# A vision tower on one core: B row split by TensorE, shares repeated by DMA, weights loaded ahead

## What is computed

```python
xn = layernorm(h); xz = xn @ W_in.T; x_main, z = split(xz)
xm = silu(conv4(x_main)); Bt = xm @ W_B.T; Ct = xm @ W_C.T
dt = softplus(xm @ W_dt.T + b_dt)                       # softplus = max(x,0) + log(1+exp(-|x|))
h[t] = exp(A*dt)*h[t-1] + dt*Bt*xm                      # 16 states, 256 channels
y = (h*Ct).sum(states); h1 = h0 + (y*silu(z)) @ W_out.T
# 8 experts, each takes its 1024 best rows of all (softmax over rows), gelu MLP, scatter-add
# last: tokens rolled by 32, attention over the 8 heads of one token (q.k of head h and head g),
#       output dealt out again and projected, then:
u = layernorm(h3); out = h3 + shared(u) + sum_e share[e] * (W_ex[e] @ swiglu(w_up @ u)) + biases
# share: one of 2 groups, the best 2 of its 4 experts, normalized
```

## Time and profile before

| | |
|---|---|
| median of three runs | 2949.59 us |
| the profiled execution | 2955.88 us, span 2954.1 us |
| busy, share of the span | PE 83%, DVE 83%, POOL 67%, ACT 51% |
| mean granted clock of TensorE | 0.924 |
| scan stage | 0 to about 1580 us |
| middle | to about 1922 us |
| last stage | to the end |

### The profile page before, as it was taken

One profiled execution on the slowest core, in us unless ns is written; L12 is line 12 of the kernel. 1 busy time (PEld: TensorE's weight loads), 2 busy tenths in 40 slices (PEclk: granted clock), 3 DMA queues, 4 the chain that ended last, 5 costly groups with the idle time before them and its releaser, 6 DMA issues. The chain is left out here.

```text
span 2954.1 us, 25221 instructions
## 1 busy us (share of the span) xinstructions
PE 2455.6 (83%) x6718; PEld 1146.3 (39%) x6718; DVE 2447.7 (83%) x3527; ACT 1511.1 (51%) x2542; POOL 1978.0 (67%) x1008
## 2 busy tenths in 40 slices
PE   6899898898998898988973068438999999998998
PEld 2344444444444444444431033213444444444443
DVE  4999999999999999999997822137888888888875
ACT  5666666666666666676652134234444433443332
POOL 3888888888888887888882068755555555555540
PEclk9999999999999999999996579758999999999999
DMA  2333323323333323324231024310000000000000
GB/s 83 110 94 98 109 92 105 106 87 117 94 99 107 100 91 108 103 87 119 89 102 51 0 50 71 36 51 22 29 29 29 29 29 29 29 29 29 26 22 11
DMA packets 169758, 199.27 MB, mean 67 GB/s; under 512 B 38969, under 2 KB 156946, under 8 KB 169490
## 3 DMA queue, kind: packets, MB, share of 16 engines
q1 hardware_dynamic: 158354, 189.27, 20.9%
q0 software_dynamic: 11264, 8.40, 2.2%
HBM read 164.37 MB, written 33.25 MB: 67 GB/s over the span
## 5 line engine op out<-in xcount | busy, mean ns | idle before, releaser
L905 POOL TENSOR_TENSOR a_hc<-a_h,a_cs 128x896 f32<-128x896 f32 (+1 forms) x448 | 891.6, 2002 | 182.1 <-DVE a_h L744 181.2
L360 PE MATMUL a_y_bank<-a_hc,a_ident 128*128 128x448 f32 (+1 forms) x1792 | 766.7, 562 | 14.7 <-POOL a_hc L905 13.6
L537 ACT ACTIVATE a_da<-a_dt,a_neg_a 128x448 f32<-128x448 f32 (+1 forms) x896 | 548.4, 632 | 331.3 <-DVE a_h L744 330.3
L744 DVE TENSOR_TENSOR_SCAN a_h<-a_da,a_h,a_dbx 128x448 f32<-128x448 f32 x528 | 583.1, 1134 | 14.2 <-ACT a_da L537 11.9
L360 PEld LDWEIGHTS a_y_bank<-a_hc,a_ident 128*128 128x128 f32 x1792 | 344.1, 196 | 359.9 <-issue 287.2
L2086 POOL TENSOR_TENSOR c_prod<-c_prob,c_qkv 128x1024 f32<-128x1024 f32 x100 | 280.7, 2849 | 274.6 <-DVE c_prob L1973 274.6
L1670 PE MATMUL c_p_ACC<-c_sc,c_w_ex 128*128 128x512 f32 x800 | 365.4, 594 | 0.0
L2079 POOL TENSOR_TENSOR c_prod<-c_qkv 128x1024 f32<-128x1024 f32 x100 | 231.9, 2341 | 152.7 <-ACT c_qkv L1754 152.7
L728 DVE TENSOR_TENSOR a_dbx<-a_dtx,a_b_bank 128x896 f32<-128x896 f32 (+1 forms) x308 | 328.5, 1067 | 4.5 <-PE a_b_bank L353 0.7
L1947 DVE TENSOR_TENSOR c_sc<-c_hid,c_p_CB 128x1024 f32<-128x1024 f32 x200 | 239.9, 1214 | 69.6 <-PE c_p_CB L1662 67.1
L893 POOL TENSOR_TENSOR a_dbp<-a_dtx,a_bs 128x896 f32<-128x896 f32 (+1 forms) x140 | 269.7, 1936 | 0.3
(11 more groups left out here) (297 smaller groups left out, 3688.3 us busy)
## 6 DMA issues: line engine op xcount, KB each, us to landing
a_cs<-c_rows SPq DMA_DIRECT2D x96, 896.0 KB, 5.3
a_bs<-c_rows SPq DMA_DIRECT2D x24, 1120.0 KB, 5.7
a_cs<-c_rows SPq DMA_DIRECT2D x16, 900.0 KB, 4.4
c_x<-h_rows SPq DMA_DIRECT2D x25, 256.0 KB, 2.8
heads<-c_ot SPq DMA_DIRECT2D x25, 256.0 KB, 2.3
c_dealt<-heads SPq DMA_DIRECT2D x200, 32.0 KB, 1.9
rolled<-c_res SPq DMA_DIRECT2D x25, 256.0 KB, 2.1
h_rows<-a_th SPq DMA_DIRECT2D x24, 224.0 KB
```

The lines of the kernel that those rows point to most:

```text
L360: pe.matmul(y_bank[:, d, 0:g.w], ident[:], hc[:, (g.i * NS + n) % HC_RING, d, 0:g.w], start=(n == 0), stop=(n == NS - 1)).then_inc(s_sum, 1)
L537: act.activation(da[:, k % DA_RING, 0:g.w], dt[g.slot][:, d, 0:g.w], ACT.Exp, scale=neg_a[:, d * NS + n:d * NS + n + 1]).then_inc(s_da, 1)
L744: dve.tensor_tensor_scan(h[:, n, d, 0:g.w], da[:, (g.i * 2 * NS + k) % DA_RING, 0:g.w], x, state, ALU.mult, ALU.add).then_inc(s_scan, 1)
L905: pool.tensor_tensor(hc[:, (q.i * NS + n) % HC_RING, :, 0:q.w], h[:, n, :, 0:q.w], cs[:, n % C_RING, 0:q.w].unsqueeze(1).to_broadcast([P, ...
```

## The change

**Scan stage.** The bank that holds B and C stays open. ScalarE rounds it to `bc` (high part); TensorE then adds minus the high part into the same bank, by a matmul with a negated identity (`less_high`); ScalarE rounds the rest (`middle_b`), TensorE takes that off too (`less_middle`), ScalarE rounds the low part (`low_b`). `split_b` and `low_b` are gone from VectorE, and `one_more` is ScalarE's. `trh` moves to bank 0, `logit` to bank 1, and all four order lists are new.

**Middle.** GpSimd clears its lists only when VectorE has made the keys. Ahead of expert 2's weights SyncE loads the last stage's weights into tiles that live through both stages (`fixed_tiles`); VectorE clears a bias tile in round 6 of the search and does the small preparations behind its middle work.

**Last stage.** The shares go to DRAM as 8 rows and come back repeated over all 128 partitions, in two transfers of 1 MB; `spread(e)` and its banks are gone. The hidden expert rows lie in PSUM (`hx`). The biases of choice and shared part are one bf16 matmul. x is transposed into the bank ahead of the projection. The order lists are new.

```diff
-              ("dt1", 0, 1), ("out", 0, -1), ("trh", 1, -1), ("cen2", 0, -1), ("var2", 1, -1), ("tok", 1, 2),
-              ("logit", 0, -1), ("cen", 0, 2), ("var", 1, 2), ("trn", 1, -1))
+              ("dt1", 0, 1), ("out", 0, -1), ("trh", 0, -1), ("cen2", 0, -1), ("var2", 1, -1), ("tok", 1, 2),
+              ("logit", 1, -1), ("cen", 0, 2), ("var", 1, 2), ("trn", 1, -1))
...
+            def less_high():
+                if p:
+                    pe.wait_ge(s_bch, p.i + 1)
+                    pe.matmul(tile_of("bc", p)[:, 0:p.w], less[:, 0, :], bc[p.slot][:, 0:p.w], start=False, stop=True,
+                              skip_group_check=True).then_inc(s_less, 1)
...
+            def low_b():
+                if p:
+                    act.wait_ge(s_less, 2 * p.i + 2)
+                    act.copy(bc[p.slot][96:128, 0:p.w], tile_of("bc", p)[96:128, 0:p.w]
+                             ).then_inc(s_free[nth["bc", p.i][0]], 1)
+
+            def one_more():
+                if p:
+                    act.wait_ge(s_spe, p.i + 1)
+                    need(act, s_spm, p.i)
+                    act.activation(yt[:, :, 0:p.w], spe[:, :, 0:p.w], ACT.Identity, bias=1.0).then_inc(s_spu, 1)
...
-            def split_b():
...
-            def low_b():
...
-            def one_more():
...
+            if e == 2:
+                progs["c_load"](sp)
             need(sp, s_out, 2 * (e - 1))
...
+            if r == 6:
+                progs["c_clear"](dve)
...
     def gpsimd(pool):
         after_a(pool)
+        pool.wait_ge(s_dve, progs["n_high"])
         pool.memset(ones[:], 1.0).then_inc(s_fill, 1)
...
+            def share_out():
+                if X is not None:
+                    sp.wait_ge(s_c_s, X + 1)
+                    sp.dma_start(share_rows[X % 2], c_s[SHARE:SHARE + E1, :]).then_inc(s_rows[X % 2], 16)
+
+            def share_in():
+                if X is not None:
+                    sp.wait_ge(s_rows[X % 2], (X // 2 + 1) * 16)
+                    for half in range(2):
...
+                        sp.dma_start(c_all[:, r, :, :], share_rows[X % 2][half * EG:(half + 1) * EG, :].partition_broadcast(P)
+                                     ).then_inc(s_all[r], 16)
+
+            load()
+            share_out()
+            heads_out()
+            store_last()
+            share_in()
+            heads_in()
...
-            def spread(e):
...
+                    product = hid[U % 2][:, i, :] if i < 2 else hx[:, i - 2, :]
...
+                    dve.tensor_tensor(sc[:, n % SC_RING, :, :], hx[:], shares(dve, X, e), ALU.mult
+                                      ).then_inc(s_sc, 1)
...
             exp_table()
+            gate_exp()
+            row_scale()
+            score_exp()
             keep_h3()
-            score_exp()
             square()
-            row_scale()
+            column_scale()
             norm_rows()
-            column_scale()
-            gate_exp()
+            affine()
             silu_table()
-            affine()
```

More of the change, by code:

```diff
@@ L1 @@
 from contextlib import ExitStack
+from dataclasses import dataclass
 import numpy as np
@@ L851, in vector @@
             scans(6, 1)
-            split_b()
+            scans(7, 0)
             product(8)
-            scans(7, 0)
             scans(7, 1)
@@ L857, in vector @@
             scans(8, 0)
+            scans(8, 1)
             product(10)
-            scans(8, 1)
             scans(9, 0)
+            scans(9, 1)
             product(11)
-            scans(9, 1)
-            one_more()
-            low_b()
-            lost()
             scans(10, 0)
@@ L1435, in bank_table @@
     return nth
-def phase_c(nc, ctx, mem, a, h_rows, out, after_b, progs):
+SHARE, PARTS = 96, (0, 32, 64)
+KB = PARTS[-1] + E1 + 1
+@dataclass
+class Fixed:
+    ident: object
+    cen_w: object
+    mean_w: object
+    w_qkv: object
+    w_proj: object
+    w_up: object
+    w_so: object
+    w_ex: object
+    w_gate: object
+    gate_b: object
+    cols: object
+    eps_cols: object
+    earlier: object
+    later: object
+    bias9: object
+    bias_b: object
+    cc: object
+    s_in: object
+    s_const: object
+    loads: int
@@ new lines, in sync, with load, store, store_last @@
+        for X, U, N, A, L in turns:
+            def load():
+                if L is not None:
+                    if L >= 3:
+                        result(sp, "proj", L - 3)
+                    sp.dma_start(x[L % 3][:], h_rows[L * GW + SHIFT:(L + 1) * GW + SHIFT, :].rearrange(
+                        "(j p) d -> p j d", p=P)).then_inc(s_x[L % 3], 16)
+            def store(c):
+                if c is not None and c >= 0:
+                    taken(sp, "acc", c)
+                    sp.dma_start(out[:, c * GW:(c + 1) * GW], res[c % 2][:]).then_inc(s_res[c % 2], 16)
+            def store_last():
+                if X:
+                    store(X - 1)
+            def heads_out():
+                if N is not None:
+                    taken(sp, "o", N)
+                    sp.dma_start(heads[N % 2], ot[:]).then_inc(s_heads[N % 2], 16)
+            def heads_in():
+                if N is not None:
+                    s = N % 2
+                    sp.wait_ge(s_heads[s], (N // 2 + 1) * 16)
+                    for j in range(8):
+                        sp.dma_start(dealt[s][j * DH:(j + 1) * DH, :, :],
+                                     heads[s][:, j, :].rearrange("(h d) c -> d h c", d=DH)).then_inc(s_dealt[s], 16)
+            def share_out():
[6 more added lines that the diff above has]
+                    for half in range(2):
+                        if X >= 2:
+                            for e in range(half * EG, half * EG + EG):
+                                scaled(sp, X - 2, e)
+                        r = X % 2 * 2 + half
+                        sp.dma_start(c_all[:, r, :, :], share_rows[X % 2][half * EG:(half + 1) * EG, :].partition_broadcast(P)
[6 more added lines that the diff above has]
+            heads_in()
```

454 lines of the change are left out of this document (223 added, 231 removed), and 8 rows, old and new, of the table BANK_ORDER.

## The result

The changed kernel takes 2866.08 us, the median of four runs (2864.81 to 2871.2), against 2951.03 us before on the same chip: ratio 0.9716, 95% interval 0.9702 to 0.9731. The time lies in the range given, 45 us above the number forecast.

| part | before | after | change | forecast |
|---|---|---|---|---|
| up to the end of the last scan | 1565.1 | 1462.7 | -102.4 | -90 |
| to the first statistics | 369.3 | 355.3 | -14.0 | -12 |
| last stage | 1019.7 | 1045.1 | **+25.4** | -27 |
| span | 2954.1 | 2863.0 | -91.1 | -129 |

What follows compares the result with a forecast made beforehand. VectorE was taken to bound the scan turn; the last stage's turn was a DRAM trip plus TensorE work. Scan -90, middle -2, boundary -10, last stage -35, last turns +8: -129 from 2949.6, 2821 us, range 2760 to 2872.

Steps and rivals of the forecast that it cites:

- Scan stage: Scan stage: VectorE sets the turn and loses three operations, 3.4 us a turn; -90 us, between -50 and -108.
- TensorE's need of 49.4: Scan stage: TensorE's work per turn, 49.0 us plus 0.4 for two added matmuls, below the new turn of 50.6.
- Rival 2: Scan stage gives half: low_b's wait passes on or TensorE loses its place; stage saves 50 us, 2861 us; 15%.
- Middle and boundary: Later memsets on GpSimd -2 us; last-stage weights loaded early, so its statistics start sooner, -10 us.
- the sum for the turn, 36.5 us: Last stage: 11.5 plus 23.8 plus 1.2 for the clock per turn; 22 full turns give -35 us.
- turn_o to project, 11.5: Last stage: the attention output's trip through DRAM, dealt delayed by the share broadcasts; 11.5 us, bounds 9.9 and 14.2.
- TensorE's part, 23.8: Last stage: TensorE's work from project to the next turn_o, 22.9 us plus 0.9 waiting for ScalarE's keep_n3.
- Clock, 1.2: Last stage: cost per turn of TensorE's clock falling behind a 2.9 us wait for dealt, 1.2 us.
- rival 3: Last stage: clock falls every turn and takes the gain; 37.9 us a turn, only -4, 2852 us; 12%.
- Rival 1: Last stage: small transfers not held up, project starts near 9.9, clock stays up; -90 us, 2766 us; 25%.
- c_rows: 84 KB transfer in the earlier trace, issued right behind a broadcast; its waiter came 5.2 us later, evidence that dealt is delayed.
- The last turns: End of last stage: nothing covers the shares' trip in the last two turns, 9.3 us against 4.7; +8 us.

Runs made afterwards that it cites:

- e7: Changed kernel with one_more back on VectorE, directly ahead of lost, and gone from ScalarE: 2888.7 us, ratio 0.9776.
- e6: Changed kernel with the scan stage (phase_a and its order table) of the kernel before: 2974.5 us, ratio 1.0069.
- e5: Kernel before with only the scan stage (phase_a and its order table) of the changed one: 2856.4 us, ratio 0.9672.
- e2: Changed kernel with the two share broadcasts cut to 4 partitions from the third group on, same order and number of transfers: 2746.2 us, ratio 0.9310.
- e9: Changed kernel with four added, unread matmuls on TensorE between the turns of x and the wait for dealt: 2828.5 us, ratio 0.9557.
- e10: Changed kernel with TensorE's projection matmul and its wait for dealt moved behind expert 0 alone: 2788.2 us, ratio 0.9432.
- e4: Changed kernel with TensorE's projection matmul and its wait for dealt moved behind experts 0 and 1: 2740.6 us, ratio 0.9291.
- e11: e4 with ScalarE's table load for silu moved behind the copy of the turned n3: 2741.3 us, ratio 0.9267.
- e12: e11 with the small share broadcasts of e2 (4 partitions from the third group on): 2731.2 us, ratio 0.9244.
- e3: Changed kernel with the three share transfers issued by ScalarE on its own queue instead of by SyncE: 2905.3 us, ratio 0.9848.

## Why the prediction was right or wrong

**Right in its range, by errors of opposite sign.** The number was 45 us low. The last stage's error, 52 us, would alone have given 2873 us, outside the range; the 12 us that the scan stage and the 2 us that the boundary gave beyond their forecasts brought the time back in. That is luck. By the sign that the prediction set itself (wrong if the last stage's turn is over 38 us) it was wrong there: the turn is 39.5.

**Scan stage: right, 12 us short.** The argument held at each step: VectorE sets the turn (e7), the three operations leave it, TensorE has room. The turn fell by 3.8 us instead of 3.4. VectorE's idle time fell as well, from 1.7 us a turn (3.1 of 100 us at 54.1; over 400 to 1400 us it is 1.4) to 0.8 (1.6 of 100 at 50.3), where I had charged 0.1 for new waits. TensorE's need of 49.4 was too high: it is 94.2% of 50.3, 47.4 us. The 49.0 from before contained stretches at the lower clock (0.97 over 400 to 1400 us, 1.00 now); by an estimate, 0.97 is half clock for 6% of the time and so at most 1.6 us of a turn. The first turn gave back 3.2 us, where I had 2. Rival 2 fell: neither `lost` nor TensorE lost its place (over 400 to 1400 us TensorE shows no wait for keep_rows or low_b).

**Middle and boundary: right**, -14.0 against -12; e6 alone gives -11.9 from its own last scan. VectorE's first two operations on x fell from 1.93 and 1.28 us (e5) to 0.57 each, 2.1 in all, where I had 2.

**Last stage: the step that failed is the sum for the turn, 36.5 us.** It measured 39.5, and all three terms were mis-sized, by about 1 us each:
- *turn_o to project, 11.5, was 12.4.* The mechanism was right (dealt 5.6 us instead of 1.9), but the second broadcast does not hide in the first one's latency. The engines are full for 8 us behind the first issue, and dealt lands when they are free. e2 gives the other end, 9.1, below my bound of 9.9.
- *TensorE's part, 23.8, was 24.9 at full clock (e9).* Not in my list was turn_o's wait of 0.48 us for ScalarE's copy of the choice, in every turn. The wait for n3's copy I had right (0.9 against 0.86). The other 0.6 us was not traced.
- *Clock, 1.2, was 2.1 (e9).* It falls in every turn, where the wait is now 4.3 us and not 2.9. This is rival 3's mechanism, and its sign (a clock under 0.95 over whole turns) is there: 0.93 over 2100 to 2500 us. It had 12%, with 2.6 us for the clock at 0.57 in every turn; in half of the turns the clock was higher than that. The last stage as a whole came out beyond its price (37.9 a turn). Rival 1 (25%) fell, as c_rows had said.

**The last turns: not as forecast.** From the choice's last product to the first scale it took 8.0 us (4.7 before, 9.3 forecast), in VectorE's timeline:

```profile
2834.51 0.16 DVE L2124 TENSOR_TENSOR c_cc<-c_share,c_p_R 128x16 f32<-128x16 f32 x1
...
2842.49 3.49 DVE L2034 TENSOR_TENSOR c_sc<-c_hx,c_c_all 128x1024 f32<-128x1024 f32 x3 [7.22 <-DMA c_c_all<-share_rows]
```

But from the last turn_o to the end it took 88.5 us, against 90.6 before: -2.1, where I had +8. What became shorter there beside the longer trip stays open. From the first turn_o on, the first two turns, in which the steps fill, took 54.9 us instead of 64.8, a gain that was not in my list; the 22 full turns behind them took 868.1 instead of 830.8, which is 37.8 a turn before and not the 38.1 that I had from 18 of them. The three parts, -9.9, +37.3 and -2.1, add up to +25.3, the table's +25.4 but for rounding.

**What the prediction did not see** is larger than its errors: it took TensorE's order as given and asked only how late dealt would be. With e9's term for the clock and the 1.8 us of an expert the change can be recomputed: with one expert ahead of the wait 39.5 - 2.1 - 1.8 = 35.6, and e10 measured 35.6; with two 33.8, and e4 measured 34.0. The second agreement is partly chance, for e4, e11 and e12 seem to stand at VectorE's limit. The expected gain of the last stage was there, and one matmul in front of ready work held it back.

## What to carry to other kernels

When a step is replaced by a large transfer, look at what else must cross the DMA engines in the same microseconds, in any queue, and at what stands behind its wait in an engine's order: here 5.5 us a turn hung on one matmul's place. A wait on TensorE is priced with the clock behind it; four useless matmuls bought back 38 us. And a total inside the range proves no step: read each part's change against its own forecast.

## What the runs showed of the hardware that I had not expected

**A transfer in its own queue is held by another queue's megabytes** (e3: 7.0 us for 256 KB, alone 2.0).

**VectorE's low_b in the kernel before waited for GpSimd.** It took 2.24 us (the mean of the 24 of 32x448), and 0.62 in the first turn (VectorE, by line: ns min/median/max, first and last start):

```profile
L778 DVE TENSOR_TENSOR a_bc<-a_bcr,a_bc x28: 624/2244/2251, 40.7 to 1497.5; 32x448 bf16<-32x448 f32 x24, 32x450 bf16<-32x450 f32 x4
```

One of them in the timeline of the kernel before:

```profile
787.59 2.24 POOL L905 TENSOR_TENSOR a_hc<-a_h,a_cs 128x896 f32<-128x896 f32 x1 [1.16 <-DVE a_h L744]
788.07 2.25 DVE L778 TENSOR_TENSOR a_bc<-a_bcr,a_bc 32x450 bf16<-32x450 f32 x1
```

It starts while GpSimd works and ends 0.49 us behind GpSimd's end (789.83). So it is in all 27 turns behind the first: 2.24 or 2.25 us, with an end 0.48 or 0.49 behind that of one of GpSimd's `weigh` operations (L905). In the first turn GpSimd is idle beside it. The Trainium skill ("SBUF — State Buffer", SBUF: two separate sides) says that a VectorE operation with two inputs in SBUF and a GpSimd operation that reads SBUF lock each other out, and the one that started first keeps the ports to its end; these rows agree. The scans read several tiles of SBUF too and keep their 1.13 us beside GpSimd (one of 1.14 us starts at 781.26, while GpSimd works from 779.24 to 783.13). No run took low_b away alone, so that its 2.24 us counted in full is worked out from the stage's sum (3.47 us removed, turn 3.8 shorter), not shown by itself.
